# Local-attention scores in two column halves of 192 keys or queries, and another order of projections in the layers' ring

## The reference

```python
valid = (delta >= 0) & (delta <= PAST_CTX)      # PAST_CTX = 125, one zero row ahead of the keys
for l in range(LAYERS):                          # 6
    keys = jnp.concatenate([past, x], axis=1)
    q = (x @ Wq.T + bq).reshape(B, T, 16, 8)     # k and v likewise, from keys
    scores = jnp.einsum('bqhd,bkhd->bhqk', q, k) / jnp.sqrt(8.)
    attn = jax.nn.softmax(jnp.where(valid, scores, neg), axis=-1)
    o = jnp.einsum('bhqk,bkhd->bqhd', attn, v).reshape(B, T, C) @ Wo[l].T + bo[l]
    x = _ln(x + o, ln1_g[l], ln1_b[l])
    ff = gelu(x @ W1[l].T + b1[l]) @ W2[l].T + b2[l]
    x = _ln(x + ff, ln2_g[l], ln2_b[l])
```

## Time and profile before

| what | value |
|---|---|
| median of 3 runs | 6034.54 us (6033.0 to 6034.73) |
| profiled execution, its own time | 6036.64 us |
| its span in the trace | 6034.9 us |
| mean granted TensorE clock | 0.86 |
| TensorE matmuls busy | 4362.9 us (72%) |
| VectorE, ScalarE, GpSimd busy | 3432.6 (57%), 2535.0 (42%), 1812.3 us (30%) |

### The profile page before, as it was taken

How to read it: one execution, slowest core, us unless ns; L and a number is a source line. 1 busy time by engine, 2 the same in 40 slices (tenths; PEclk the granted TensorE clock), 3 DMA queues, 4 the chain that set the end, 5 groups by cost and what they waited for, 6 DMA issues and landing times.

```text
span 6034.9 us, 103008 instructions
## 1 busy us (share of the span) xinstructions
PE 4362.9 (72%) x33740; PEld 2635.8 (44%) x33740; DVE 3432.6 (57%) x15760; ACT 2535.0 (42%) x5084; POOL 1812.3 (30%) x3770
## 2 busy tenths in 40 slices
PE   3469999999999999926399899960000017998999
PEld 3435555555555555526144377730000003444776
DVE  2266666666666666521466512139999985663111
ACT  1236666666666666613155433330000003553333
POOL 2345565565655556531422200000000001221000
PEclk9779999999999999958599889985555557997999
DMA  5300000000000000015100000020000000000000
GB/s 137 107 11 2 2 10 2 5 6 2 10 2 10 2 5 2 1 41 155 35 2 2 1 3 0 0 97 0 0 0 0 0 11 1 2 2 1 1 0 14
DMA packets 118045, 103.17 MB, mean 17 GB/s; under 512 B 20496, under 2 KB 94512, under 8 KB 117168
## 3 DMA queue, kind: packets, MB, share of 16 engines
q1 hardware_dynamic: 113456, 88.61, 5.1%
q0 software_dynamic: 4096, 8.40, 0.5%
HBM read 74.82 MB, written 22.15 MB: 16 GB/s over the span
## 4 chain that ended last, share of the span: by engine, by line
PE 62%; DVE 18%; ACT 9%; issue 5%; POOL 4%; DMA 1%; SPq 0%; POOLq 0%; DVEq 0%; ACTq 0%; PEldq 0%
PE ps L1526 8%; PE ps L1516 7%; PE ps L1205 6%; PE ps L1195 6%; PE ps L1243 5%; PE ps L1400 4%; PE ps L1388 4%; PE ps L1175 3%; PE ps L1086 3%; ACT arena L1743 3%; PE ps L1185 3%; DVE arena L2578 3%; DVE arena L2556 2%; ACT arena L1761 2%; PE ps L1429 2%
## 5 line engine op out<-in xcount | busy, mean ns | idle before, releaser
L2081 DVE CUSTOM_DVE_ANT_0 arena<-ps,mask_win 128x256 f32<-128x256 f32 (+1 forms) x3072 | 1011.3, 387 | 454.3 <-PE ps L1195 443.3
L1743 ACT ACTIVATE arena<-ps 128x512 f32<-128x512 f32 (+1 forms) x1536 | 754.4, 544 | 598.8 <-PE ps L1205 597.0
L1205 PE MATMUL ps<-arena 32*128 32x512 f32 (+1 forms) x3072 | 873.6, 589 | 16.6 <-ACT arena L1743 10.1
L1195 PE MATMUL ps<-arena 32*128 32x256 f32 (+1 forms) x6144 | 834.6, 381 | 39.8 <-ACT arena L1716 38.6
L1195 PEld LDWEIGHTS ps<-arena 32*128 32x128 f32 x6144 | 494.8, 185 | 324.9 <-issue 102.5
L1526 PEld LDWEIGHTS ps<-w,arena 128*128 128x128 f32 x4096 | 535.2, 191 | 231.5 <-issue 229.4
L1671 PE MATMUL ps<-arena,ones 128*128 128x342 f32 x16 | 9.0, 737 | 865.6 <-DVE arena L2592 862.2
L2253 DVE CUSTOM_DVE_ANT_0 arena<-ps,mask_cau 128x512 f32<-128x512 f32 (+3 forms) x1024 | 450.0, 488 | 307.9 <-PE ps L1388 279.1
L1908 ACT ACTIVATE arena<-ps,eb 128x512 f32<-128x512 f32 x512 | 351.8, 687 | 559.8 <-PE ps L1516 559.8
L2300 DVE SCALAR_TENSOR_TENSOR X<-ps,C,X 128x128 f32 (+1 forms) x512 | 144.3, 344 | 772.5 <-PE ps L1526 772.3
L895 POOL TENSOR_SCALAR_AFFINE_SELECT arena<-arena 128x1024 f32<-128x1024 f32 x384 | 419.9, 1093 | 544.8 <-ACT arena L1743 531.0
(11 more groups left out here) (305 smaller groups left out, 8102.2 us busy)
## 6 DMA issues: line engine op xcount, KB each, us to landing
w<-in_L_w_dram SPq DMA_DIRECT2D x160, 256.0 KB
arena<-xs SPq DMA_DIRECT2D x10, 512.0 KB, 6.5
ys<-arena SPq DMA_DIRECT2D x10, 512.0 KB, 4.3
xs<-zero SPq DMA_DIRECT2D x1, 2560.0 KB, 11.2
w<-in_L_w_dram SPq DMA_DIRECT2D x1, 2048.0 KB
scr_k<-arena SPq DMA_DIRECT2D x8, 256.0 KB, 2.1
scr_v<-arena SPq DMA_DIRECT2D x8, 256.0 KB, 2.3
scr_f<-arena SPq DMA_DIRECT2D x8, 256.0 KB, 2.3
```

Of the source, the lines that this page charges most:

```text
L1195: return pe.matmul(ps[:, bank, s.at(v):s.at(v) + s.kw], Q[p][r][rows, v, s.tile * P:(s.tile + 1) * P], K[p][r][rows, s.k0:s.k0 + s.kw], st ...
L1205: pe.matmul(ps[:, bank, 0:2 * t.w].rearrange("p (v q) -> p v q", q=t.w), K[p][r][rows, t.k0:t.k0 + P], Q[p][r][rows, 0:2, t.q0:t.q0 + t.w] ...
L1743: act.activation(PTs[m % L.SLOTS][:, k * w:(k + 1) * w], bank[:, 0:w], exp, scale=-1.0)\
L2081: x = dve.tensor_tensor_reduce(out=seen, in0=bank[:, s.at(v):s.at(v) + s.kw], in1=mask, scale=1.0, scalar=NO_SCORE, op0=ALU.add, op1=ALU.m ...
```

## The change

Each score matmul becomes two: queries 0 to 63 of the tile against the window's columns 0 to 191, and queries 64 to 127 against columns 64 to 255 (the padded item: columns 0 to 65 and 0 to 129). They write partitions 0 to 63 and 64 to 127 of the bank, so they lie on different column groups of the array. Each turned score becomes two in the same way: 64 keys each, with 192 queries of each v. The signal stands on the second one. In the ring zT, k 0, q 0 and q 1 get other places, the projections' wait for zT stands at both k 0 and q 0, and the first scores of a unit wait for its queries as well as its keys.

```diff
-            uses += {(0, 0, 1): [("A", "zT", n)], (0, 1, 1): [("A", "q", n, 0)], (0, 2, 1): [("A", "k", n, 0)],
-                     (0, 3, 0): [("A", "q", n, 1)], (1, 0, 1): [("A", "k", n, 1)],
+            uses += {(0, 0, 0): [("A", "zT", n)], (0, 0, 1): [("A", "k", n, 0)], (0, 1, 1): [("A", "q", n, 0)],
+                     (0, 2, 1): [("A", "q", n, 1)], (1, 0, 1): [("A", "k", n, 1)],
                      (1, 1, 1): [("A", "v", n)]}.get(at, [])
...
-                    if k == 0 and r == 0:
+                    if r == 0:
                         consumed_a("zT", n)
...
-                    return pe.matmul(ps[:, bank, s.at(v):s.at(v) + s.kw],
-                                     Q[p][r][rows, v, s.tile * P:(s.tile + 1) * P],
-                                     K[p][r][rows, s.k0:s.k0 + s.kw], start=True, stop=True, skip_group_check=True)
+                    for h in range(2):
+
+                        lo, hi = (0, KPAD + 64 * (h + 1)) if s.padded else (64 * h, 64 * h + 192)
+                        q0 = s.tile * P + 64 * h
+                        m = pe.matmul(ps[64 * h:64 * h + 64, bank, s.at(v) + lo:s.at(v) + hi],
+                                      Q[p][r][rows, v, q0:q0 + 64], K[p][r][rows, s.k0 + lo:s.k0 + hi],
+                                      start=True, stop=True, skip_group_check=True)
+                    return m
...
-                    pe.matmul(ps[:, bank, 0:2 * t.w].rearrange("p (v q) -> p v q", q=t.w),
-                              K[p][r][rows, t.k0:t.k0 + P], Q[p][r][rows, 0:2, t.q0:t.q0 + t.w],
-                              start=True, stop=True, skip_group_check=True).then_inc(L.a_done, 1)
+                    out = ps[:, bank, 0:2 * t.w].rearrange("p (v q) -> p v q", q=t.w)
+                    for h in range(2):
+
+                        lo, hi = 64 * h, min(64 * h + 192, t.w)
+                        m = pe.matmul(out[64 * h:64 * h + 64, :, lo:hi], K[p][r][rows, t.k0 + lo:t.k0 + lo + 64],
+                                      Q[p][r][rows, 0:2, t.q0 + lo:t.q0 + hi], start=True, stop=True,
+                                      skip_group_check=True)
+                    m.then_inc(L.a_done, 1)
...
                             consumed_a("k", n, r)
+                            consumed_a("q", n, r)
```

## The result

The changed kernel takes 5889.83 us (median of 4 runs, 5888.95 to 5892.28) against 6034.64 for the kernel before (6033.0 to 6035.71): a ratio of 0.9761, 95% interval 0.9744 to 0.9778, or 145 us less. The forecast was 5861, its own range 5835 to 5895. The profiled execution spans 5887.2 us, 147.7 less than before.

What follows compares the result with a forecast made beforehand. TensorE, with holes in it, was taken as the bound. Savings of 3.05 us (even unit) and 0.7 (odd unit) make 3.75 a stage, 165 over 44 stages, plus 9: 174 us less, 5861 us, range 5835 to 5895.

Steps and rivals of the forecast that it cites:

- The bound and the holes: TensorE bounds the layer phase, busy 43.45 of 45.61 us a stage, with holes waiting for keys' and queries' copies.
- The half bracket: Four scores beside two turned scores on TensorE; split, a full one falls from 1.07 to about 0.81 us.
- Full overlap of the column halves: Both column halves of split matmuls run side by side; the rival of no overlap, chance 0.07, gave 6195 us.
- Issue at nothing: Issuing 24 records per half bracket costs nothing; the rival at 55 ns a record, chance 0.03, gave 6218 us.
- The order: Moved projections close two TensorE holes, 0.96 and 0.89 us: 1.85 us a stage; rival of order alone, chance 0.10, 5945.
- The ring of three banks then finds its bank free at (0,3,1): With queries 1 copied one bracket earlier, TensorE finds a free bank there; part of closing the 1.85 us of holes.
- What is given back: Two long brackets a stage still wait for ScalarE, with GpSimd holding one; of 5.15 us a stage 3.75 stays.
- Counting only TensorE's work and the holes: Rival that the ScalarE and GpSimd chains give way: 5.15 us a stage, 247 in all, 5787 us; chance 0.18.
- The even unit: Part of a stage whose long bracket waits for ScalarE's exps, apply and sums: 3.05 us saved a stage.
- The odd unit: Part of a stage where GpSimd's root, with 0.36 us margin, holds ScalarE's apply: 0.7 us saved a stage.
- The clock: TensorE's granted clock was read as 1.00, its 2.4 GHz level, from 600 to 1000 us; no loss was counted.
- The sum: 3.75 us a stage over 44 stages, 165, plus 9 for the first three: 174 us less, giving 5861.

Runs made afterwards that it cites:

- order_only: The kernel before with only the new order of zT, keys 0, queries 0 and queries 1, matmuls unsplit: 5968.99 us, ratio 0.9896.
- split_only: The kernel before with only the split of scores and turned scores, its order kept: 5949.58 us, ratio 0.9864.
- wide_halves: The changed kernel with both column halves streaming the whole window (256 or 2 x w columns) instead of 192: 5945.92 us, ratio 0.9858.
- root_early: The changed kernel with GpSimd's second root moved between the masks of items 0 and 1 of the even unit: 5857.71 us, ratio 0.971.
- root_early_rows_late: The changed kernel with GpSimd's second root moved into the even unit and its affine rows behind the masks of item 2: 5840.95 us, ratio 0.9681.
- keys_early: The changed kernel with queries 1 put back behind the small bracket (0,3,0), the other moves kept: 5931.91 us, ratio 0.9833.
- apply_late: The changed kernel with ScalarE's apply behind the exps of (.,2,0) and GpSimd's affine rows behind the masks of item 2: 5803.24 us, ratio 0.9623.
- all_moved: The changed kernel with GpSimd's second root early, its affine rows late and ScalarE's apply late together: 5736.28 us, ratio 0.9507.

## Why the prediction was right

*The bound and the holes.* Right. TensorE was the bound; `order_only` and `split_only` both gain, and their gains add.

*The half bracket.* Right. 0.81 was forecast for a full one, 0.83 measured; 0.60 and 0.61 for a small one. Full overlap of the column halves, chosen between bounds of 0.81 and 1.44, is what the chip does, and `wide_halves`, with 1.04, shows that the time follows their columns. The weight loads do not stand in the way: 0.83 us leaves no room for three more exposed loads. The rule of the Trainium skill that a load overlaps only on another row group ("TensorE: Matmul & The Clock Gate", Part 3, what overlaps and what doesn't), weighed in the prediction, does not hold here. One sign failed: TensorE's busy share was forecast at some 90% and is 96% (40.52 of 42.10 us, before 95%): its busy time fell by 2.93 us, nearly as much as the stage.

*Issue at nothing.* Right. 24 records in 0.83 us are 35 ns each, well under the 55 of the densest window before, and the small half bracket has 24 in 0.61 us: 25 ns a record, 51 ns for each of its 12 matmul instructions. The figure of about 62 ns a matmul that the Trainium skill gives for software decode ("TensorE: Matmul & The Clock Gate", section on 56 against 53.3 ns) does not apply here, counted by record or by instruction.

*The order.* The mechanism was right, a term too large: 1.85 us a stage forecast, 1.40 measured. "The ring of three banks then finds its bank free at (0,3,1)" is true of that bracket, which takes 0.61 us (1264.79 to 1265.40). The step that failed is its silent extension to the brackets around it: TensorE comes to (0,3,0) and (1,0,0) sooner, before ScalarE has freed the bank of their second turned scores, and they stretch by 0.15 and 0.2. The last 0.1 us a stage was not traced.

*What is given back.* Right, and the part that made the number. Counting only TensorE's work and the holes gave 5787. The even unit, measured from the bracket (0,0,0) to (1,0,0), went from 1411.79 to 1435.61, 23.82 us, to 20.74 (1245.25 to 1265.99): 3.08 saved, 3.05 forecast. Its parts fit too: 0.42 lost in front of (0,1,0) where 0.54 was forecast, 0.49 saved from there to V (5.85 us instead of 6.34) where 0.46 was, and 3.01 behind it where 3.27 was. The odd unit saved 45.61 - 23.82 - (42.10 - 20.74) = 0.43, where 0.7 was forecast; the stretch of (1,0,0), 0.19, is most of the difference. The reason stands as given: GpSimd's root ends at its fixed distance from the exps of the last unit, and the apply waits for it. Moving the root early shortened (1,2,0) by 0.49 us but by itself gained nothing a stage; with the affine rows and the apply moved too, the stage fell from 42.10 to 39.41, 2.7 us. With these chains out of the way the gain is 296 us instead of 145. That is more than the 247 of TensorE's own sum, because the two long brackets of the kernel before shrink as well.

*The clock.* Missing. The prediction had read a granted clock of 1.00 through the layers and carried it over, a term at nothing. In 13 of the 44 stages it falls to 0.50 for 3.4 us, and such a stage is 1.6 us longer: about 20 us in all. Without them the change would have given about 5870, an estimate. The dips begin always in the same place, about 4 us after the values' projection, behind the long bracket (1,2,0) and its idle stretch. The runs differ in the length of that stretch:

| kernel | longest idle of TensorE in the 6 us from the values' projection, median us | full stages with a dip |
|---|---|---|
| before, `order_only`, `wide_halves` | 0.13, 0.13, 0.22 | 0 |
| `root_early`, `root_early_rows_late` | 0.54, 0.55 | 0 |
| `keys_early` | 0.92 | 11 |
| `split_only` | 0.94 | 16 |
| changed kernel | 1.04 | 13 |
| `apply_late` (in front of V) | 1.47 | 1 |

`all_moved` has no such stretch and no dip. So the dips come with the longer stretches, but their length alone does not decide: most stages of the changed kernel with the same 1.04 us have none, and `apply_late`, with more, has one. No run parts the stretch from the split, and what else decides stays open.

*The sum.* 3.51 us a stage against 3.75 forecast, and the dips, make the 29 us between 5861 and 5890; the first three stages (15.6 instead of 9) and the phases after the layers (4.7 lost) nearly cancel, which is luck. The measured 5890 lies 5 us inside the upper end of the range.

## What to carry to other kernels

When a change shortens the busiest engine's work, walk the queue of each other engine through one period before counting the gain: here TensorE's own sum promised 5.15 us a stage, and 3.51 came. Most of the rest was held by a ScalarE chain that already had no slack and a GpSimd chain that had 0.36 us. The remedy was not a faster instruction but another place for three pieces of work: the root, the affine rows and the apply. And split matmuls into column halves for all that should run together, or for none: half a split cost 461 us, the whole one gained 145.

## What the runs showed of the hardware that I had not expected

- Tiles of 32 x 64 and of 32 x 128 on different row groups do not overlap: a full half bracket of both shapes takes 2.03 or 2.07 us, one of either shape alone 0.83 to 1.07. With the new order of projections, and against the kernel before, splitting only the scores costs 461 us where splitting both kinds gains 145.
- The two column halves of a row group run side by side, on four row groups at once: 0.83 us for a full half bracket whose halves stream different windows of 192 columns, and 1.04 with 256 columns each, where four tiles of 32 x 128 took 1.07.
- 24 f32 matmul records start within 0.61 us in a small half bracket, 25 ns each.
- With TensorE busy 96% of a stage (40.52 of 42.10 us) its granted clock still fell to 0.50 for 3.4 us in 13 of 44 stages, behind idle stretches of about 1.04 us such as the one in front of 1275.34; with 0.54 us of idle there (`root_early`) it did not.
